# A convolution-and-transformer kernel: the 16-bit high part of the first activation is written by ScalarE instead of VectorE

## The chip, the core and the metric

One core of one Trainium2 chip runs the whole program. The metric is device time in microseconds (us), taken as the median of several executions. Busy times, starts and waits come from one profiled execution of the same kernel.

## What is computed

The program has two parts. The first turns 784 patches of 16x16 pixels with 3 colours (16 images of 7x7 patches) into tokens with a small residual convolution network; the second runs attention and MLP blocks over the tokens. The change touches the first part only:

```python
# 784 patches (bsz*h0*w0), each 3 x 16 x 16, normalized by its own mean and std
x = _conv2d(x, conv1_w, conv1_b)              # 3 -> 64 channels, 3x3
residual = x
x = _group_norm(x, gn1_g, gn1_b)              # 32 groups
x = jax.nn.gelu(x, approximate=False)         # <- the first activation
x = _conv2d(x, rconv1_w, rconv1_b)            # 64 -> 64 channels, 3x3
x = _group_norm(x, gn2_g, gn2_b)
x = jax.nn.gelu(x, approximate=False)
x = _conv2d(x, rconv2_w, rconv2_b)
x = residual + x
x = _conv2d(x, proj_w, proj_b, stride=P, pad=0)   # 64*16*16 -> 192 per patch
```

All is float32 in the reference. The kernel keeps the accuracy by splitting values into a 16-bit high part and a 16-bit low part, so that TensorE multiplies 16-bit numbers.

## The kernel before

**Stages.** From 0 to some 213 us the last convolution and the projection are folded into one matrix and the images are laid out. From some 213 to 1220 us the main stage runs over all patches. The rest, to 1526 us, is the tail with its transformer blocks. The change lies in the main stage.

**Tiling of the main stage.** A unit is 8 patches and there are 98 units. A unit has two halves q = 0, 1 of 4 patches each. A half is a *slot*, numbered k = 2u + q, so 196 slots; 14 units (28 slots) form a group, and there are 7 groups. The 128 partitions hold 64 channels times the two halves (even and odd rows) of a patch, and a slot's activation is 128 x 512 (4 patches x 128 pixels). Loops over pairs of units repeat the same four slots.

**One slot on each engine**, in the order in which the engine's own instruction list has it:

- TensorE (`emit`, L633): 30 matmuls of the 64 -> 64 convolution of slot k, in 15 pairs that use the two halves of the array at once. It first waits until the low part for slot k is there (`s_sp1`), after 6 pairs until the doubled high part has landed (`s_dup`), after 10 pairs it multiplies the statistics of slot k+3 (`means`, L602, waits for `s_ms`), after 13 pairs it does the first convolution (`conv1`, L592) into the bank that the gelu of slot k+2 must have left (`s_g1`). In all groups but the first the projection of the group before (`project`, L611) is woven between the pairs, from the fifth slot of the group on.
- VectorE (`slot`, L880): statistics of the two results (`channel_stats`, two times 4 instructions, L837), `moments` (L844 to L849), the low part of the second activation (`split2`, L877), `read_means` (L853 to L858), and last `split1` for slot k+2 (L868 and L870).
- GpSimd (`norm`, L388): turns the means into a scale and a shift for each patch, five small instructions (L394 to L404), of which the first is a power.
- ScalarE (`pair`, L489): the gelu of the second activation of slot k-3 (`gelu2_at`, 4 instructions, L477), its 16-bit high part (`hi2`, L485), and the gelu of the first activation of slot k+2 (`gelu1`, 4 instructions, L469). Each gelu needs a scale and shift of `norm`; the one of slot n of the first and the one of slot n-4 of the second use the same `norm(n)`.
- SyncE's queue (`double`, L292): four DMAs for a slot that copy the high part `hst[q]` into both partition halves of `acts[p]`, since every channel half is needed with both row halves. Between the slots stand loads of the image (`load_im`), of the projection's low weights (`load_chunk`), and at a group's end the stores of tokens.

**The split of the first activation.** The gelu writes `g1f` (float32). `split1` writes its 16-bit copy `hi` into `hst[q]`, with a border of zeros around each patch (rows of 16 written into rows of 18), signals `s_sp1h` (the doubling DMAs wait for it), and then writes `lo = g1f - hi` into `acts[p]`, which signals `s_sp1`:

```python
dve.wait_ge(s_g1, k + 1)                               # the gelu of slot k is done
if doubled is not None:
    dve.wait_ge(s_dup[1 - p][q], 64 * doubled)         # hst[q]'s last content has been copied on
v.tensor_copy(hi, src).then_inc(s_sp1h, 1)             # L868
dve.wait_ge(s_sp1h, k + 1)
v.tensor_tensor(lo, src, hi, ALU.subtract).then_inc(s_sp1, 1)   # L870
```

There are 198 such splits: 196 slots and two beyond the last.

Of the kernel before, what the change touches and what calls it, by code (L numbers as in the profile page):

```python
# [20 lines left out]
ALU, ACT = mybir.AluOpType, mybir.ActivationFunctionType  # L21

B, C, P, CH, E = 16, 3, 16, 64, 192
# [3 lines left out]
SL, WD = 9, 18  # L27
# [3 lines left out]
Q = 4  # L31
UNITS = NPAT // U
GU = 14
# [38 lines left out]
def build_front(nc, a, emb, xs, ts, wrd):  # L72
# [9 lines left out]
    with ExitStack() as ctx:  # L82
# [15 lines left out]
        g1f = f32q[:, 0:U * HALF].rearrange("p (g n) -> p g n", g=U)  # L98
        acts = [sb(f"acts_{i}", [128, 3, HB], F16) for i in range(2)]
        hfull = sb("hst", [128, U * PAD], F16)  # L100
        hst = [hfull[:, q * Q * PAD:(q + 1) * Q * PAD] for q in range(2)]
# [63 lines left out]
        s_scr, s_zero, s_padz = sem("x_stored"), sem("zero_tile"), sem("pads_zeroed")  # L165
# [258 lines left out]
        @block.scalar  # L424
        def _(act):
            def proj_hi(i, p, wait=True):
                n = 2 * i + p
                act.wait_ge(s_pld[p], 16 * (i + 1))
                if wait:
                    act.wait_ge(s_psp, n)  # L430
                    act.wait_ge(s_fdup, 64 * n)
                nc.scalar.activation(hfull[:, :].rearrange("p (r x) -> p r x", x=WD * Q)[:, :, Q:(P + 1) * Q],
                                     stage[p].rearrange("p (r x) -> p r x", x=P * Q), ACT.Copy, scale=WS).then_inc(s_psh, 1)

            def fold_step(i, p, first, more=True):
                n = 2 * i + p
                for q in range(2):
                    act.wait_ge(s_fold, 2 * n + q + 1)
                    nc.scalar.activation(whi[:, :, bass.ds(n * U + q * Q, Q)],
                                         rc[p][q][:, :].rearrange("p (n e) -> p n e", e=Q),  # L440
                                         ACT.Copy, scale=1.0 / WS).then_inc(s_whi, 1)
                if more:
                    proj_hi(i + 1, p)
                if not first:
                    act.wait_ge(s_ts[p], 32 * i)
                act.wait_ge(s_tps, n + 1)
                for k, bank in enumerate((c1[0], c1[1], pj)):
                    nc.scalar.activation(tev[p][:, :, 3 * P * k:3 * P * (k + 1)],
                                         bank[:, 0:192].rearrange("p (n e) -> p e n", e=Q),
                                         ACT.Copy, scale=1.0 / (WS * WS)).then_inc(s_tev, 1)  # L450

            act.wait_ge(s_padz, 2)
            proj_hi(0, 0, False)
            proj_hi(0, 1)
            for p in range(2):
                fold_step(0, p, True)
            with act.Fori(1, FU // 2 - 1) as i:
                for p in range(2):
                    fold_step(i, p, False)
            for p in range(2):  # L460
                fold_step(FU // 2 - 1, p, False, False)

            def gelu1(k, q, guard=True):

                act.wait_ge(s_sh, k + 1)
                if guard:
                    act.wait_ge(s_sp1, k - 1)
                for m in range(Q):
                    ins = nc.scalar.activation(g1f[:, q * Q + m, :], c1[q][:, m * HALF:(m + 1) * HALF], ACT.Gelu,  # L469
                                               bias=gsh[q][:, m:m + 1], scale=gsc[q][:, m:m + 1])  # L470
                ins.then_inc(s_g1, 1)

            def gelu2_at(u, q, p):
                act.wait_ge(s_sh, 2 * u + q + 5)
                act.wait_ge(s_sp2, 2 * u + q + 1)
                for m in range(Q):
                    ins = nc.scalar.activation(g2f[:, q * Q + m, :], rc[p][q][:, m * HALF:(m + 1) * HALF], ACT.Gelu,  # L477
                                               bias=gsh[q][:, Q + m:Q + m + 1],
                                               scale=gsc[q][:, Q + m:Q + m + 1])
                ins.then_inc(s_g2, 1)  # L480

            def hi2(u, q, buf, slot):

                act.wait_ge(s_g2, 2 * u + q + 5)
                nc.scalar.activation(g2[buf][:, 0, bass.ds(slot, Q), :], g2f[:, q * Q:q * Q + Q, :],  # L485
                                     ACT.Copy).then_inc(s_sp2h, 1)

            def group(g, b, first):
                def pair(u0, j, first, head):  # L489
                    for p in range(2):  # L490
                        u = u0 + p
                        for q in range(2):

                            if not (first and 2 * p + q < 3):
                                if head and 2 * p + q == 3:
                                    act.wait_ge(s_pj, 1 if first else g)
                                uu, qq, pp = (u - 2, 1, p) if q == 0 else (u - 1, 0, 1 - p)
                                gelu2_at(uu, qq, pp)
                                old = head and 2 * p + q < 3
                                hi2(uu, qq, 1 - b if old else b, slot2(j, p, q, old))  # L500
                            gelu1(2 * u + 2 + q, q)

                pair(g * GU, 0, first, True)
                with act.Fori(1, GU // 2) as j:
                    pair(g * GU + 2 * j, j, False, False)

            act.sem_inc(s_g2, 4)
            gelu1(0, 0, False)
            gelu1(1, 1, False)
            group(0, 0, True)  # L510
            act.wait_ge(s_wst, 16)
            with act.Fori(0, (GROUPS - 1) // 2) as i:
                group(2 * i + 1, 1, False)
                group(2 * i + 2, 0, False)
            for k in range(2 * UNITS - 3, 2 * UNITS):
                gelu2_at(k // 2, k % 2, k // 2 % 2)
                hi2(k // 2, k % 2, 0, (2 * GU + k - 2 * UNITS) * Q)
# [199 lines left out]
        def _(dve):  # L717
            v = nc.vector
# [138 lines left out]
                dve.wait_ge(s_mv, 2 * n + 2)  # L857
                v.tensor_tensor(mst[s][:, 1, :], mst[s][:, 1, :], msm[s][:, :], ALU.subtract).then_inc(s_rd, 1)  # L858

            def split1(k, q, p, doubled):  # L860

                dve.wait_ge(s_g1, k + 1)
                if doubled is not None:
                    dve.wait_ge(s_dup[1 - p][q], 64 * doubled)
                src = g1f[:, q * Q:q * Q + Q, :].rearrange("p g (r w) -> p g r w", w=P)
                hi = hst[q][:, :].rearrange("p (g r w) -> p g r w", g=Q, r=SL)[:, :, 1:9, 1:17]
                lo = acts[p][:, 2, q * Q * PAD:(q + 1) * Q * PAD].rearrange("p (g r w) -> p g r w", g=Q, r=SL)[:, :, 1:9, 1:17]
                v.tensor_copy(hi, src).then_inc(s_sp1h, 1)  # L868
                dve.wait_ge(s_sp1h, k + 1)
                v.tensor_tensor(lo, src, hi, ALU.subtract).then_inc(s_sp1, 1)  # L870

            def split2(k, q, buf, slot):
# [6 lines left out]
            def group(g, b, first):  # L879
                def slot(u, q, p, j, head, first):  # L880

                    pair_at = g * (GU // 2) + j

                    k = 2 * u + q
                    seen = not (first and p == 0 and q == 0)
                    if seen:
                        dve.wait_ge(s_rc, k)
                        channel_stats(1 - q, rc[p][0] if q == 1 else rc[1 - p][1], Q)
                    dve.wait_ge(s_c1, k + 5)
                    channel_stats(1 - q, c1[1 - q], 0)  # L890
                    moments(k + 3, 1 - q, 11 * k + 25 if seen else 25)
                    if not (first and p == 0) and not (first and p == 1 and q == 0):
                        old = head and 2 * p + q < 3
                        split2(k - 3, 1 - q, 1 - b if old else b, slot2(j, p, q, old))
                    read_means(k + 3, 1 - q)
                    split1(k + 2, q, 1 - p, pair_at + 1)

                def pair(u0, j, first, head):
                    for p in range(2):
                        for q in range(2):  # L900
                            if head and p == 1 and q == 1:
                                dve.wait_ge(s_pj, g if not first else 1)
                            slot(u0 + p, q, p, j, head, first)

                pair(g * GU, 0, first, True)
                with dve.Fori(1, GU // 2) as j:
                    pair(g * GU + 2 * j, j, False, False)
# [15 lines left out]
            moments(1, 1, 11)  # L923
            read_means(0, 0)
            read_means(1, 1)
            split1(0, 0, 0, None)
            dve.wait_ge(s_c1, 4)
            channel_stats(0, c1[0], 0)
            moments(2, 0, 18)
            read_means(2, 0)  # L930
            split1(1, 1, 0, None)
            group(0, 0, True)
            dve.wait_ge(s_wst, 16)
            with dve.Fori(0, (GROUPS - 1) // 2) as i:
# [747 lines left out]
```

## Time and profile before

| what | us |
|---|---|
| median of 3 runs | 1520.43 |
| lowest and highest of them | 1519.85, 1529.87 |
| the profiled execution | 1527.82 |
| its span, first to last instruction | 1526.0 |
| mean granted TensorE clock in it | 0.964 of full |
| PE (matmul) busy | 1378.1 (90%) |
| DVE (VectorE) busy | 1119.1 (73%) |
| ACT (ScalarE) busy | 860.6 (56%) |
| POOL (GpSimd) busy | 583.2 (38%) |

Busy times are those of the whole span. Since the stages differ, a share over the span says little about one stage; the rows further down are therefore cut by stage. "Idle before" an instruction is put down to what its engine waited for last. The names of engines in rows are PE (matmul), PEld (weight load), DVE, ACT, POOL and SPq (SyncE's queue).

### The profile page before, as it was taken

Reading aid. Unit: us, or ns where it says so; the run is one execution under the profiler, and the core shown is the slowest. Engines: PE = TensorE matmul, PEld = TensorE weight load, DVE = VectorE, ACT = ScalarE, POOL = GpSimd, SP = SyncE. Lnnn points to the kernel's source line nnn. Section 1 sums busy time; section 2 is a strip of 40 time slices with the busy share of each in tenths; the row PEclk is TensorE's granted clock in tenths of the full one; section 3 lists DMA queues with packets and bytes.
Section 4 is the critical chain, followed back from the end, with each engine's and each line's share of the span. In section 5 each row is a group of like instructions: output and inputs, shape, how many; then the busy total and the mean of one; then the engine's idle time right before and its main releaser. Section 6 shows DMA issues by size and latency. Waiting matters only on the chain. (4 is left out here: it accounts for less than half of the span.)

```text
span 1526.0 us, 43786 instructions
## 1 busy us (share of the span) xinstructions
PE 1378.1 (90%) x14026; PEld 1022.3 (67%) x14026; DVE 1119.1 (73%) x4210; ACT 860.6 (56%) x2126; POOL 583.2 (38%) x1114
## 2 busy tenths in 40 slices
PE   3999959888999999989999998999999785978889
PEld 1877523334888588768867885888578675655647
DVE  5753338999888988888898887888988743475630
ACT  1333426777676776667767676676666601333451
POOL 1000025555545545445454554544545401152600
PEclk9999979999999999999999999999999987977999
DMA  7899863334554555455545554555455596400000
GB/s 209 238 260 261 232 240 102 99 98 125 140 147 132 136 142 144 111 143 147 145 124 148 141 144 111 144 146 133 135 141 144 147 252 152 92 1 1 2 0 17
DMA packets 124565, 206.95 MB, mean 136 GB/s; under 512 B 19964, under 2 KB 88124, under 8 KB 123774
## 3 DMA queue, kind: packets, MB, share of 16 engines
q1 hardware_dynamic: 124414, 204.89, 49.8%
q8 instruction: 100, 1.64, 0.5%
q14 instruction: 51, 0.42, 0.1%
HBM read 103.70 MB, written 21.30 MB: 82 GB/s over the span
## 5 line engine op out<-in xcount | busy, mean ns | idle before, releaser
L540 PE MATMUL rc<-sb_acts,sb_rwd 128*64 128x512 f16 x1764 | 562.7, 392 | 20.2 <-DMA sb_acts<-sb_hst 19.5
L541 PE MATMUL rc<-sb_acts,sb_rwd 128*64 128x512 f16 x1764 | 563.7, 392 | 0.0
L394 POOL TENSOR_TENSOR sb_tmp<-sb_mst,sb_half_neg 128x8 f32<-128x8 f32 x200 | 353.9, 1770 | 471.5 <-DVE sb_mst L858 471.5
L469 ACT ACTIVATE sb_f32q<-c,sb_gsh,sb_gsc 128x128 f32<-128x128 f32 x792 | 298.3, 458 | 285.3 <-POOL sb_gsh L404 285.3
L540 PE MATMUL rc<-sb_acts,sb_rwl 128*64 128x512 f16 x1176 | 364.2, 392 | 5.3 <-issue 5.3
L541 PE MATMUL rc<-sb_acts,sb_rwl 128*64 128x512 f16 x1176 | 363.6, 391 | 0.0
L619 PE MATMUL pj<-sb_wall_arena 128*64 128x384 f16 x1792 | 306.0, 335 | 12.7 <-DVE sb_wall_arena L877 6.6
L477 ACT ACTIVATE sb_g2f<-rc,sb_gsh,sb_gsc 128x128 f32<-128x128 f32 x784 | 297.4, 482 | 4.5 <-POOL sb_gsh L404 4.5
L623 PEld LDWEIGHTS pj<-sb_wall_arena 128*64 128x64 f16 x1792 | 218.2, 223 | 66.1
L623 PE MATMUL pj<-sb_wall_arena 128*64 128x192 f16 x1792 | 238.7, 246 | 0.0
L540 PEld LDWEIGHTS rc<-sb_acts,sb_rwd 128*64 128x64 f16 x1764 | 179.8, 110 | 82.8 <-DMA sb_acts<-sb_hst 29.7
L619 PEld LDWEIGHTS pj<-sb_wall_arena 128*64 128x64 f16 x1792 | 215.0, 219 | 29.7 <-DMA sb_wall_arena<-w_lo 6.9
L560 PE MATMUL rc<-sb_acts,sb_wall_arena 128*64 128x512 f16 x720 | 165.5, 386 | 24.7 <-DVE sb_acts L748 15.2
L541 PEld LDWEIGHTS rc<-sb_acts,sb_rwd 128*64 128x64 f16 x1764 | 179.7, 110 | 5.1
L837 DVE BATCH_NORM_STATS2 sb_bn<-rc 128x6 f32<-128x128 f32 x784 | 173.7, 283 | 12.4 <-issue 5.4
L837 DVE BATCH_NORM_STATS2 sb_bn<-c 128x6 f32<-128x128 f32 x800 | 174.2, 278 | 0.0
L561 PE MATMUL rc<-sb_acts,sb_wall_arena 128*64 128x512 f16 x720 | 164.9, 385 | 0.0
L540 PEld LDWEIGHTS rc<-sb_acts,sb_rwl 128*64 128x64 f16 x1176 | 126.7, 109 | 48.6 <-issue 10.9
L877 DVE TENSOR_TENSOR sb_wall_arena<-sb_g2f,sb_wall_arena 128x512 f32 (+1 forms) x196 | 135.6, 692 | 31.0 <-issue 16.9
L870 DVE TENSOR_TENSOR sb_acts<-sb_f32q,sb_hst 128x512 f16<-128x512 f32 x198 | 137.8, 696 | 6.8
L485 ACT ACTIVATE sb_wall_arena<-sb_g2f 128x512 f32 (+1 forms) x196 | 124.8, 637 | 27.8 <-ACT sb_g2f L477 9.4
L541 PEld LDWEIGHTS rc<-sb_acts,sb_rwl 128*64 128x64 f16 x1176 | 126.7, 109 | 0.5
(171 smaller groups left out, 1888.2 us busy)
## 6 DMA issues: line engine op xcount, KB each, us to landing
sb_acts<-sb_hst SPq DMA_DIRECT2D x792, 78.8 KB, 2.6
sb_im<-x_planes SPq DMA_DIRECT2D x202, 136.5 KB
sb_wall_arena<-w_lo SPq DMA_DIRECT2D x48, 528.0 KB, 3.8
sb_acts<-sb_hst SPq DMA_DIRECT2D x96, 162.0 KB, 3.1
sb_wall_arena<-w_lo SPq DMA_DIRECT2D x24, 480.0 KB, 3.7
sb_f32q<-in_proj SPq DMA_DIRECT2D x12, 576.0 KB, 4.6
sb_wall_arena<-in_proj SPq DMA_DIRECT2D x12, 576.0 KB, 4.7
w_lo<-sb_wall_arena SPq DMA_DIRECT2D x1, 6144.0 KB, 20.7
```

The costliest lines, as they stand in the source:

```text
L394: ch.did(gp.tensor_tensor(t1, var, half_neg[:, :], ALU.pow))
L469: ins = nc.scalar.activation(g1f[:, q * Q + m, :], c1[q][:, m * HALF:(m + 1) * HALF], ACT.Gelu, bias=gsh[q][:, m:m + 1], scale=gsc[q][:, m ...
L477: ins = nc.scalar.activation(g2f[:, q * Q + m, :], rc[p][q][:, m * HALF:(m + 1) * HALF], ACT.Gelu, bias=gsh[q][:, Q + m:Q + m + 1], scale= ...
L540: nc.tensor.matmul(out[0:CH, :], w_odd, x_odd, start=(n == 0), stop=(n == 14))
L541: yield nc.tensor.matmul(out[CH:128, :], w_even, x_even, start=(n == 0), stop=(n == 14))
L560: nc.tensor.matmul(out[0:CH, :], w_odd, x_odd, start=(n == 0), stop=(n == 14))
L561: yield nc.tensor.matmul(out[CH:128, :], w_even, x_even, start=(n == 0), stop=(n == 14))
L619: last = nc.tensor.matmul(pj[at:at + 64, 0:2 * E], g2[b][:, 0, k:k + 64, n], both, start=(n == 0), stop=False)
L623: last = nc.tensor.matmul(pj[at:at + 64, 0:E], g2[b][:, 1, k:k + 64, n], whi[:, n, :], start=False, stop=(n == HALF - 1))
L837: v.bn_stats(bn6[s][:, at + m, :], src[:, m * HALF:(m + 1) * HALF]).then_inc(s_dch, 1)
L870: v.tensor_tensor(lo, src, hi, ALU.subtract).then_inc(s_sp1, 1)
L877: v.tensor_tensor(lo, src, hi, ALU.subtract).then_inc(s_sp2, 1)
```

## The change

The copy into `hst[q]` leaves `split1` and becomes a function of ScalarE, `hi1`, which follows each `gelu1`. The wait for the DMAs that read `hst[q]` (`s_dup`) goes with it. VectorE's `split1` keeps the subtraction only and waits for ScalarE's signal `s_sp1h` where it waited for the gelu. At the start ScalarE waits until the borders are zeroed.

```diff
+            def hi1(k, q, p, doubled):
+                if doubled is not None:
+                    act.wait_ge(s_dup[1 - p][q], 64 * doubled)
+                act.wait_ge(s_g1, k + 1)
+                src = g1f[:, q * Q:q * Q + Q, :].rearrange("p g (r w) -> p g r w", w=P)
+                nc.scalar.activation(hst[q][:, :].rearrange("p (g r w) -> p g r w", g=Q, r=SL)[:, :, 1:9, 1:17], src,
+                                     ACT.Copy).then_inc(s_sp1h, 1)
...
                             gelu1(2 * u + 2 + q, q)
+                            hi1(2 * u + 2 + q, q, 1 - p, g * (GU // 2) + j + 1)
...
             act.sem_inc(s_g2, 4)
+            act.wait_ge(s_padz, 2)
+            act.wait_ge(s_zl, 3)
             gelu1(0, 0, False)
+            hi1(0, 0, 0, None)
             gelu1(1, 1, False)
+            hi1(1, 1, 0, None)
...
-            def split1(k, q, p, doubled):
+            def split1(k, q, p):
 
-                dve.wait_ge(s_g1, k + 1)
-                if doubled is not None:
-                    dve.wait_ge(s_dup[1 - p][q], 64 * doubled)
+                dve.wait_ge(s_sp1h, k + 1)
                 src = g1f[:, q * Q:q * Q + Q, :].rearrange("p g (r w) -> p g r w", w=P)
...
-                v.tensor_copy(hi, src).then_inc(s_sp1h, 1)
-                dve.wait_ge(s_sp1h, k + 1)
                 v.tensor_tensor(lo, src, hi, ALU.subtract).then_inc(s_sp1, 1)
```

## Rows read from the trace of the kernel before

**Rows 1.** Windows, group 0 and groups 1 to 6: length, busy by engine, clock, DMA.

```profile
235.00:375.00 140.00, 123.90 (x1090) 53.21 (x1090) 129.43 (x543) 103.74 (x266) 75.48 (x150) 1.00 0.41 103
375.00:1211.00 836.00, 811.15 (x8978) 651.02 (x8978) 732.76 (x2964) 581.61 (x1480) 414.15 (x821) 0.99 0.51 138
```

**Rows 2.** The same windows, line L868 (VectorE's copy) alone: length, busy, count.

```profile
235.00:375.00 140.00, 12.83 (x30) 1.00 0.41 103
375.00:1211.00 836.00, 70.10 (x165) 0.99 0.51 138
```

**Rows 3.** Waits, 235 to 371 us: who waited for whom, us, times, longest.

```profile
PEld st L607 <- DVE sb_ms L849: 25.1, 29, 1.2
PEld c L598 <- ACT sb_f32q L469: 15.9, 26, 1.0
```

**Rows 4.** Waits, 371 to 1210 us.

```profile
PEld rc L540 <- DMA sb_acts<-sb_hst: 19.0, 23, 3.3
...
PEld st L607 <- DVE sb_ms L849: 13.6, 15, 1.4
```

**Rows 5.** Groups by line: names, shapes, count, busy us, mean ns, idle before.

```profile
L485 ACT ACTIVATE sb_wall_arena<-sb_g2f 128x512 f32 (+1 forms) x196 | 124.8, 637 | 27.8 <-ACT sb_g2f L477 9.4
L868 DVE CAST sb_hst<-sb_f32q 128x512 f16<-128x512 f32 x198 | 84.3, 426 | 3.8 <-ACT sb_f32q L469 3.3
...
L432 ACT ACTIVATE sb_hst<-sb_f32q 128x1152 f16<-128x1152 f32 x12 | 13.9, 1156 | 1.7 <-DMA sb_acts<-sb_hst 1.7
```

**Rows 6.** Timeline, 282 to 292 us (group 0): start, length, engine, line, idle before.

```profile
282.17 0.17 DVE L858 TENSOR_TENSOR sb_mst<-sb_mst,sb_msm 128x8 f32<-128x8 f32 x1
...
282.42 1.75 POOL L394 TENSOR_TENSOR sb_tmp<-sb_mst,sb_half_neg 128x8 f32<-128x8 f32 x1 [1.90 <-DVE sb_mst L858]
...
282.71 0.69 DVE L870 TENSOR_TENSOR sb_acts<-sb_f32q,sb_hst 128x512 f16<-128x512 f32 x1
...
283.75 0.63 ACT L485 ACTIVATE sb_wall_arena<-sb_g2f 128x512 f32 x1 [0.22 <-ACT sb_g2f L477]
...
285.17 1.50 ACT L469 ACTIVATE sb_f32q<-c,sb_gsh,sb_gsc 128x128 f32<-128x128 f32 x4 [0.79 <-POOL sb_gsh L404]
...
286.83 0.17 DVE L858 TENSOR_TENSOR sb_mst<-sb_mst,sb_msm 128x8 f32<-128x8 f32 x1
...
287.41 0.69 DVE L870 TENSOR_TENSOR sb_acts<-sb_f32q,sb_hst 128x512 f16<-128x512 f32 x1
...
290.08 1.50 ACT L469 ACTIVATE sb_f32q<-c,sb_gsh,sb_gsc 128x128 f32<-128x128 f32 x4 [1.25 <-POOL sb_gsh L404]
```

**Rows 7.** Timeline, 856 to 864 us (group 4), ScalarE and VectorE.

```profile
856.30 1.50 ACT L469 ACTIVATE sb_f32q<-c,sb_gsh,sb_gsc 128x128 f32<-128x128 f32 x4 [1.18 <-POOL sb_gsh L404]
...
858.51 0.42 DVE L868 CAST sb_hst<-sb_f32q 128x512 f16<-128x512 f32 x1
...
858.97 0.70 DVE L870 TENSOR_TENSOR sb_acts<-sb_f32q,sb_hst 128x512 f16<-128x512 f32 x1
...
859.34 0.64 ACT L485 ACTIVATE sb_wall_arena<-sb_g2f 128x512 f32 x1
...
861.52 1.51 ACT L469 ACTIVATE sb_f32q<-c,sb_gsh,sb_gsc 128x128 f32<-128x128 f32 x4 [1.54 <-POOL sb_gsh L404]
...
862.05 0.69 DVE L877 TENSOR_TENSOR sb_wall_arena<-sb_g2f,sb_wall_arena 128x512 f32 x1
...
863.97 0.70 DVE L870 TENSOR_TENSOR sb_acts<-sb_f32q,sb_hst 128x512 f16<-128x512 f32 x1
```

**Rows 8.** Timelines of GpSimd and VectorE, 250 to 256 us (group 0).

```profile
254.20 1.64 POOL L394 TENSOR_TENSOR sb_tmp<-sb_mst,sb_half_neg 128x8 f32<-128x8 f32 x1 [1.49 <-DVE sb_mst L858]
...
254.36 0.43 DVE L868 CAST sb_hst<-sb_f32q 128x512 f16<-128x512 f32 x1 [0.24 <-ACT sb_f32q L469]
```

**Rows 9.** Timeline of SyncE's queue, 645 to 656 us (start of group 3).

```profile
649.17 5.05 SPq L296 DMA_DIRECT2D sb_acts<-sb_hst  x8
```

**Rows 10.** Timeline of VectorE, 650 to 652 us (start of group 3).

```profile
651.14 0.43 DVE L868 CAST sb_hst<-sb_f32q 128x512 f16<-128x512 f32 x1
```

More of the change, by code:

```diff
@@ L880, in slot @@
                 def slot(u, q, p, j, head, first):
-                    pair_at = g * (GU // 2) + j
                     k = 2 * u + q
@@ L895, in slot @@
                     read_means(k + 3, 1 - q)
-                    split1(k + 2, q, 1 - p, pair_at + 1)
+                    split1(k + 2, q, 1 - p)
                 def pair(u0, j, first, head):
@@ L925, in _ @@
             read_means(1, 1)
-            split1(0, 0, 0, None)
+            split1(0, 0, 0)
             dve.wait_ge(s_c1, 4)
@@ L930, in _ @@
             read_means(2, 0)
-            split1(1, 1, 0, None)
+            split1(1, 1, 0)
             group(0, 0, True)
```

## The prediction

> **What bounds the kernel now.** I read the windows by stage first, then the waits in each, then the timeline of single slots. Only the main stage holds the edited instructions, and it has two regimes. In group 0 (235 to 375 us) there is no projection to weave in: 30 copies lie in 140 us, so a slot takes 140 / 30 = 4.67 us [rows 2], VectorE is busy 129.43 of 140 us (92%) and TensorE 123.90 [rows 1]. There TensorE waits for VectorE's statistics (25.1 us in 29 waits) and for the first gelu (15.9 us in 26) [rows 3]. In groups 1 to 6 (375 to 1211 us) a slot takes 836 / 165 = 5.07 us [rows 2], and TensorE is busy 811.15 of 836 us (97%), VectorE 732.76 (88%), ScalarE 581.61 (70%) [rows 1]. TensorE's statistics wait is down to 13.6 us over 165 slots, and its largest wait is for the doubling DMAs, 19.0 us [rows 4]. So TensorE sets the slot in 165 of some 196 slots, and what VectorE gains or loses there is cover. ScalarE idles 1.18 and 1.54 us ahead of its first gelu there [rows 7]: room for one more instruction.
>
> The reader should not take the 92% in group 0 for the whole answer. Behind it stands a loop with latency that spans two slots: `read_means(n)` on VectorE, `norm(n)` on GpSimd, `gelu1(n)` on ScalarE, `split1(n)` on VectorE, then VectorE's statistics, moments, `split2`, and `read_means(n+2)`. Its pieces in group 0 [rows 6]: end of L858 at 282.17 + 0.17 = 282.34 to the gelu at 285.17 is 2.83 us, the next time 287.00 to 290.08 = 3.08; mean 2.95. The gelu takes 1.50. From the start of L870 (282.71) to the end of the next L858 (287.00) is 4.29, all of it VectorE work. What is left of two slots, 9.33 - 2.95 - 1.50 - 4.29 = 0.59 us, is the time from the gelu's end to the start of L870: the copy of 0.43 and small gaps. The loop is almost tight before the change.
>
> **Removed on VectorE.** The copy: 426 ns x 198 = 84.3 us of busy time [rows 5]. In groups 1 to 6 this lies beside a TensorE at 97%, so it is worth nothing by itself. In group 0 it would be worth 0.43 x 30 = 12.8 us if nothing took its place.
>
> **Added on ScalarE.** The trace has no Copy from `g1f` into `hst` by ScalarE. The nearest row is `hi2`, the same size and function, 637 ns [rows 5]. The padded destination can be judged from L432, which writes that same tile with borders: 1152 elements in 1156 ns [rows 5]. The step from 512 to 1152 elements is 519 ns for 640, or 0.81 ns an element, with no sign of a price for borders. So I take 0.64 us; the lower end is 0.60 and the upper end 1.16, the whole of L432's row. Before it comes the wait for the gelu's own end, as before `hi2`: 0.22 us [rows 6]. So the high part is there 0.86 us after the gelu's end, where VectorE had it 0.43 us after it at best.
>
> **ScalarE's own cycle.** In the main stage it works from 856.30 to 859.34 + 0.64 = 859.98, that is 3.68 us, and starts again at 861.52 [rows 7]. With 0.22 + 0.64 added it works 4.54 us of 5.07 and is free at 860.84, still 0.68 us before its next gelu. So the first gelu is not delayed, nor is TensorE's `conv1` behind it. Behind the new instruction on ScalarE stand `gelu2` and `hi2`, for which VectorE's `split2` and, a slot later, TensorE wait; they come 0.86 us later. VectorE's `split2` (L877) started at 862.05, 2.07 us behind the end of `hi2` at 859.98 [rows 7], so they stay hidden. If that cover were gone, each 0.1 us would cost 16.5 us over 165 slots.
>
> **The moved wait.** `s_dup` asks for the DMAs of two slots earlier. TensorE passes the same semaphore in mid-slot, before VectorE's `read_means`, so VectorE never waited for it. ScalarE meets it up to a microsecond earlier. It costs nothing except where the DMAs are late for TensorE too (23 waits, 19.0 us [rows 4]), and there the slot is already lost. No DMA is added, and SyncE's queue keeps its order.
>
> **Groups 1 to 6, regular slots.** Gelu ends at 857.80, high part at 858.66, L870 can start 0.08 us later (the gap with which POOL follows L858, 282.34 to 282.42 [rows 6]), at 858.74; it started at 858.97 [rows 7]. The next slot: 863.03 + 0.94 = 863.97, the same as before [rows 7]. So VectorE neither gains nor loses; the bill there is 0. The high part itself is ready at 858.66 instead of 858.93, or in the other slot 863.89; the doubling DMAs follow within some tenths of the old time and are needed more than a slot later.
>
> **Starts of groups 1 to 6.** Behind the tokens' stores SyncE's queue is late and issues eight doublings back to back, 649.17 to 654.22 [rows 9]. VectorE's copy in this stretch ran at 651.14 to 651.57 [rows 10], and the second four issues followed it at once. If VectorE's copy stood directly behind the gelu, the high part now comes later by 0.86 - 0.43 = 0.43 us, and TensorE is waiting for these DMAs (up to 3.3 us [rows 4]). Six starts x 0.43 = +2.6 us; the bounds are 0, where the queue is the later one, and twice that.
>
> **Group 0.** The loop becomes 2.95 + 1.50 + (0.22 + 0.64 + 0.08) + 4.29 = 9.68 us for two slots, 4.84 a slot. One term may shrink: GpSimd's power starts just after VectorE's copy and takes 1.75 us [rows 6]; the one at 254.20 takes 1.64, and there the copy began only at 254.36 [rows 8]. With the copy gone and VectorE idle at that moment, I take 1.64: 9.57, or 4.785 a slot. Cost: (4.785 - 4.67) x 30 = +3.5 us; +5.2 with the power as it is. VectorE alone could go at 4.67 - 0.43 = 4.24, but it now waits some 0.5 us a slot at L870.
>
> The Trainium skill (GPSIMD Engine Reference, Key points) says that GpSimd shares its SBUF interfaces with VectorE and contends with instructions in a 2-port mode or with two SBUF inputs. By that rule the power gets its 1.64 us only while L870, which has two SBUF inputs, is not running; the power at 254.20 had the copy beside it and was short, so the start seems to matter, not the overlap. By the rule in full the sum would be the +5.2, by the row +3.5.
>
> **Sum.** 3.5 + 2.6 = +6.1 us. Against the profiled execution (1527.82, of which 1526.0 is span) that is 1533.9; it was 7.4 us longer than the median, so for the median 1520.43 + 6.1 = 1526.5 us.
>
> **The rivals.**
>
> *VectorE's relief carries.* If the high part were no later for VectorE than before, group 0 falls by up to 12.8 us, and the shorter VectorE slot also takes some of the 13.6 us of statistics waits. For it: VectorE at 92%, TensorE's 25.1 us of waits. Against: the loop above, which has 0.59 us for what now needs 0.94. Time: 1520.4 - 12.8 = 1507.6, still within 1%; only with most of the 13.6 us added does it pass 1% (15.2 us). 12%.
>
> *ScalarE becomes the bound (slower).* The place is ScalarE's cycle. It decides when that cycle s passes the point where 165 (s - 5.07) + 30 (s - 4.67) = 15.2, which is s = 5.09, a Copy of 0.64 + (5.09 - 4.54) = 1.19 us, or a small Copy and 0.5 us of waits. At 0.1 us more, s = 5.19: +19.8 + 15.6 = +35, 1556. Against: both Copy rows fit 0.81 ns an element. 7%.
>
> *The doubling DMAs come late everywhere.* If the later high part in the slots with little slack delays landings that TensorE waits for, a price of 0.4 us in half of the 165 slots is +33; more likely in the 23 places that already wait: 23 x 0.4 = +9, with group 0 1533. For: the waits exist. Against: in 142 of 165 slots TensorE finds the DMAs landed [rows 4]. 11%.
>
> **How the numbers follow.** The forecast has 70%, with its own range from 1520 (no cost: the power and the hand-over both shorter) to 1531 (5.2 + 2.6, and 2.4 for a Copy of 0.8 us). The rest is 12, 7 and 11%. The range over all, holding 8 in 10, goes from 1511 to 1539: it leaves out the full relief and ScalarE as the bound. About 1% is what a measurement of this kernel can tell from no change: faster by over 1% (below 1505.2) 4%, the strongest part of the relief; slower by over 1% (above 1535.6) 12%, ScalarE's case and half of the DMAs'; within 1% 84%.
>
> **What would show each step right or wrong.** The new ScalarE row at 0.60 to 0.68 us, 198 times, behind an idle of about 0.2 us. L870 in group 0 with a new wait for ScalarE, about 0.5 us in each slot, and a group 0 slot of 4.75 to 4.85 us. VectorE's busy time down by 84 us, ScalarE's up by 126. TensorE still at 97% from 375 to 1211 us, with slots of 5.07 to 5.10. The power at 1.64 us. Wrong would be: group 0 slots under 4.6 us (the loop does not bind), ScalarE with no wait for GpSimd left (it is the bound), or TensorE's waits for the doubling DMAs well above 30 us.

## The result

| | before | after |
|---|---|---|
| median, us | 1522.3 (10 runs, 1517.15 to 1529.95) | 1538.05 (10 runs, 1532.97 to 1540.25) |
| profiled execution, us | 1527.82 | 1538.50 |
| ratio | | 1.0089, 95% interval 1.007 to 1.0108 |

The changed kernel is slower: by 0.9% (13.5 us) in the ratio, by 15.75 us in the medians. The forecast was 1526.5 us, +6.1 us. Its direction was right and its size less than half of the measured one. The median of 1538.05 us lies outside the forecast's own range (1520 to 1531) and just inside the range over all (1511 to 1539). Part of that distance is the starting point: the forecast was added to 1520.43 us, and over all ten runs the kernel before has a median of 1522.3.

The two profiled executions differ by 10.7 us only. That is because the one of before was a long one: from the last subtraction to the last projection matmul it took 59.7 us, but 51.4 us in the changed kernel and 51.5 to 55.6 us in the kernels of the experiments. Up to the last subtraction of the main stage (1211.1 us before, 1227.9 after) the changed kernel is 16.8 us longer, and there lies the loss.

Windows of the kernel after, all engines: length, busy (count) of PE, PEld, DVE, ACT, POOL, clock, DMA share, GB/s.

```profile
235.00:375.00 140.00, 116.21 (x1030) 52.46 (x1028) 112.00 (x483) 113.95 (x278) 76.34 (x141) 0.99 0.37 93
375.00:1211.00 836.00, 802.70 (x8856) 639.56 (x8854) 666.54 (x2777) 676.46 (x1629) 423.72 (x815) 1.00 0.51 137
```

The same windows, the subtraction (L879) alone:

```profile
235.00:375.00 140.00, 19.44 (x28) 0.99 0.37 93
375.00:1211.00 836.00, 112.93 (x163) 1.00 0.51 137
```

Against [rows 1, 2]: in group 0 28 splits instead of 30 in 140 us, so 5.0 us a slot instead of 4.67; in the rest 163 instead of 165. VectorE is down from 129.4 to 112.0 us and from 732.8 to 666.5, in part because fewer slots lie in these windows. Over the whole span its busy time fell by 72.0 us (1119.1 to 1047.1), not by the 84 us of the copy's row, since neighbouring instructions overlap at their edges. The relief is there, and it has bought nothing.

Groups by line, kernel after; they answer to [rows 5] and [rows 6]:

```profile
L478 ACT ACTIVATE sb_hst<-sb_f32q 128x512 f16<-128x512 f32 x198 | 127.5, 644 | 21.8 <-DMA sb_acts<-sb_hst 4.0
L879 DVE TENSOR_TENSOR sb_acts<-sb_f32q,sb_hst 128x512 f16<-128x512 f32 x198 | 137.2, 693 | 77.3 <-ACT sb_hst L478 75.5
L394 POOL TENSOR_TENSOR sb_tmp<-sb_mst,sb_half_neg 128x8 f32<-128x8 f32 x200 | 366.3, 1832 | 469.5 <-DVE sb_mst L871 469.5
```

ScalarE's copy takes 644 ns, as forecast, and VectorE now waits 75.5 us for it. The new thing is the third row: GpSimd's power, untouched by the change, takes 1832 ns in the mean instead of 1770, where 1640 was forecast. The mean hides two populations: 106 powers of 1.64 or 1.65 us and 94 of 2.01 to 2.19 us. Of the 94, 93 meet the subtraction L879. The last power of the kernel meets the other subtraction instead, the one of the second activation, and the kernel before has the same case at the same place, the only one of its 200 powers above 1.91 us:

```profile
1215.80 1.29 DVE L877 TENSOR_TENSOR sb_wall_arena<-sb_g2f,sb_wall_arena 128x512 f16<-128x512 f32 x2
```

```profile
1215.96 2.02 POOL L394 TENSOR_TENSOR sb_tmp<-sb_mst,sb_half_neg 128x8 f32<-128x8 f32 x1 [2.54 <-DVE sb_mst L858]
```

Timeline of one pair of slots in group 0, kernel after, columns as in [rows 6]:

```profile
304.02 0.17 DVE L871 TENSOR_TENSOR sb_mst<-sb_mst,sb_msm 128x8 f32<-128x8 f32 x1
...
304.27 1.64 POOL L394 TENSOR_TENSOR sb_tmp<-sb_mst,sb_half_neg 128x8 f32<-128x8 f32 x1 [1.14 <-DVE sb_mst L871]
...
305.51 0.70 DVE L879 TENSOR_TENSOR sb_acts<-sb_f32q,sb_hst 128x512 f16<-128x512 f32 x1 [1.32 <-ACT sb_hst L478]
...
306.78 0.20 POOL L404 TENSOR_TENSOR sb_gsh<-sb_wid,sb_tmp 128x8 f32<-128x8 f32 x1
307.08 0.63 ACT L493 ACTIVATE sb_wall_arena<-sb_g2f 128x512 f32 x1 [0.22 <-ACT sb_g2f L485]
307.62 1.49 ACT L469 ACTIVATE sb_f32q<-c,sb_gsh,sb_gsc 128x128 f32<-128x128 f32 x4
...
309.20 0.64 ACT L478 ACTIVATE sb_hst<-sb_f32q 128x512 f16<-128x512 f32 x1
309.63 0.17 DVE L871 TENSOR_TENSOR sb_mst<-sb_mst,sb_msm 128x8 f32<-128x8 f32 x1
...
309.87 0.69 DVE L879 TENSOR_TENSOR sb_acts<-sb_f32q,sb_hst 128x512 f16<-128x512 f32 x1
309.88 2.18 POOL L394 TENSOR_TENSOR sb_tmp<-sb_mst,sb_half_neg 128x8 f32<-128x8 f32 x1 [2.90 <-DVE sb_mst L871]
```

Slots no longer follow each other evenly: subtractions start 4.36 us apart (305.51 to 309.87), then 5.6 to 6.2. In the first slot VectorE waits 1.32 us for the high part. In the second the shift is ready at 306.98, but ScalarE is in `hi2` until 307.71 and the gelu starts 0.64 us late; the high part then comes just as VectorE ends its means, the subtraction starts at 309.87, the power at 309.88, and the power takes 2.18 us. In the following, such a power is called hit.

Waits, 375 to 1211 us, kernel after; they answer to [rows 4]:

```profile
DVE sb_acts L879 <- ACT sb_hst L478: 51.7, 83, 1.9
...
PEld rc L553 <- DMA sb_acts<-sb_hst: 23.5, 30, 2.9
PEld c L611 <- ACT sb_f32q L469: 14.0, 14, 1.8
```

In the following, a group's length is the time from one subtraction's start to that of the 28th after it (for the last group, to the last one, the 27th).

| us | group 0 | groups 1 to 6 | together |
|---|---|---|---|
| before | 130.7 | 849.2 | 979.9 |
| after | 139.5 | 857.7 | 997.2 |

Of groups 1 to 6, the slots 9 to 22 of each took 426.2 us before and 426.3 after. The 8.5 us are lost in the first eight slots (240.7 to 246.0) and the last six (182.3 to 185.4).

### The profile page after: what moved, and what is told of

Its sections match the earlier page's. It is cut to its first block and busy times, and to the rows that moved or that the text cites. A ratio compares the mean times of both kernels' runs of the same rounds, so it can differ in the third digit from the quotient of the medians.

```text
span 1536.7 us, 43835 instructions
## 1 busy us (share of the span) xinstructions
PE 1383.5 (90%) x14026; PEld 1018.6 (66%) x14026; DVE 1047.1 (68%) x4012; ACT 982.9 (64%) x2324; POOL 601.9 (39%) x1114
## 3 DMA queue, kind: packets, MB, share of 16 engines
q8 instruction: 100, 1.64, 0.5%
## 5 line engine op out<-in xcount | busy, mean ns | idle before, releaser
L394 POOL TENSOR_TENSOR sb_tmp<-sb_mst,sb_half_neg 128x8 f32<-128x8 f32 x200 | 366.3, 1832 | 469.5 <-DVE sb_mst L871 469.5
L485 ACT ACTIVATE sb_g2f<-rc,sb_gsh,sb_gsc 128x128 f32<-128x128 f32 x784 | 291.0, 451 | 3.7 <-POOL sb_gsh L404 3.5
L636 PEld LDWEIGHTS pj<-sb_wall_arena 128*64 128x64 f16 x1792 | 220.4, 223 | 66.5
L632 PEld LDWEIGHTS pj<-sb_wall_arena 128*64 128x64 f16 x1792 | 219.6, 219 | 22.2 <-DVE sb_wall_arena L886 6.7
L879 DVE TENSOR_TENSOR sb_acts<-sb_f32q,sb_hst 128x512 f16<-128x512 f32 x198 | 137.2, 693 | 77.3 <-ACT sb_hst L478 75.5
L553 PEld LDWEIGHTS rc<-sb_acts,sb_rwl 128*64 128x64 f16 x1176 | 127.2, 109 | 50.1 <-issue 13.5
L478 ACT ACTIVATE sb_hst<-sb_f32q 128x512 f16<-128x512 f32 x198 | 127.5, 644 | 21.8 <-DMA sb_acts<-sb_hst 4.0
```

The lines of the kernel that those rows point to most:

```text
L394: ch.did(gp.tensor_tensor(t1, var, half_neg[:, :], ALU.pow))
L553: nc.tensor.matmul(out[0:CH, :], w_odd, x_odd, start=(n == 0), stop=(n == 14))
L632: last = nc.tensor.matmul(pj[at:at + 64, 0:2 * E], g2[b][:, 0, k:k + 64, n], both, start=(n == 0), stop=False)
L636: last = nc.tensor.matmul(pj[at:at + 64, 0:E], g2[b][:, 1, k:k + 64, n], whi[:, n, :], start=False, stop=(n == HALF - 1))
```

## The experiments

**Group 0 alone, and groups 1 to 6 alone.** Which stage pays? In the first run ScalarE copies in group 0 and ahead of it, in the second in groups 1 to 6.

```diff
-                            hi1(2 * u + 2 + q, q, 1 - p, g * (GU // 2) + j + 1)
+                            if zero:          # first run; "if not zero" in the second
+                                hi1(2 * u + 2 + q, q, 1 - p, g * (GU // 2) + j + 1)
...
+                    split1(k + 2, q, 1 - p, g * (GU // 2) + j + 1, not zero)   # VectorE copies elsewhere; "zero" in the second
```

> The new arrangement (ScalarE copies) in group 0 and ahead of it only, VectorE copies as before in groups 1 to 6. Theory A (two losses: group 0 is a loop bound by latency, where the changed kernel's trace has 4.98 us a slot instead of 4.67, and the starts of the other groups lose 1 to 3 us each): group 0 takes some 139 us again instead of 131, groups 1 to 6 their old lengths, the whole +8 us, ratio 1.005 to 1.006. Theory B (the loss is ScalarE's fuller schedule everywhere, mostly in groups 1 to 6): under +3 us, ratio 1.002 or less.

Measured: ratio 1.0035 (1.002 to 1.005); group 0 139.4 us, groups 1 to 6 847.2.

> The other part alone: VectorE copies in group 0, ScalarE copies in groups 1 to 6. Theory A: group 0 back at 131 us; in groups 1 to 6 the regular slots stay at 10.1 us a pair and only the first slots of each group are later, 8 us together, ratio 1.004 to 1.006. Theory B: most of the 13 to 16 us is here, ratio 1.009. The prediction had +2.6 us for this part.

Measured: ratio 1.0025 (1.0008 to 1.0042); group 0 131.0 us, groups 1 to 6 854.4 (slots 9 to 22: 426.4). Both parts pay, group 0 8.7 us and the others 5.2 here and 8.5 in the changed kernel. Theory A was right that there are two losses and that the middle slots pay nothing beside a busy TensorE. Its ratios were high by 0.15% or more, and it had the second loss in the first slots of a group only, where the last six take part (182.3 to 184.2 us). The two ratios together give 0.6% where the whole change gave 0.9%; the intervals just allow it.

**A gap in front of the subtraction.** In the changed kernel the hit powers all belong to subtractions that start at or before the power. A fill of a spare tile by VectorE should move the subtraction behind the power's start.

```diff
             def split1(k, q, p):
+                v.memset(dum[:, :], 0.0)      # 128x256 float32; 128x400 in the second run
                 dve.wait_ge(s_sp1h, k + 1)
```

> The changed kernel with a fill of 128x256 (0.27 us by VectorE's other fills) put ahead of VectorE's wait for the high part. In the changed kernel's trace GpSimd's power takes 1.64 us where VectorE's subtraction starts 0.1 us or more behind the power's start, and 2.02 to 2.19 us where the subtraction is already running. Theory A (this collision is part of the loss): with the gap all powers take 1.64 to 1.76 us and group 0 falls from 139.5 to 135 us or less although VectorE does 0.27 us more in each slot; ratio to before 1.004 to 1.006. Rival (the collision is only a mark, the late high part is the whole cost): the powers get shorter, group 0 stays at 139 us or grows, ratio 1.009 or more.

Measured: ratio 1.0144 (1.0109 to 1.0178), group 0 139.9 us. The expected gain did not come, and the reason stands in the timeline of this kernel:

```profile
309.85 0.27 DVE L876 MEMSET sb_dum<- 128x256 f32 x1
310.04 0.63 DVE L881 TENSOR_TENSOR sb_acts<-sb_f32q,sb_hst 128x512 f16<-128x512 f32 x1
```

```profile
309.93 2.23 POOL L395 TENSOR_TENSOR sb_tmp<-sb_mst,sb_half_neg 128x8 f32<-128x8 f32 x1 [2.90 <-DVE sb_mst L872]
```

With the fill directly ahead of it the subtraction hits the power although it starts 0.11 us behind the power's start: 90 powers took 2.23 us. So this edit made the collision worse and cannot say what the kernel is without it.

> As the gap before, with a fill of 128x400 instead of 128x256. The first gap (0.19 us in effect) put the subtraction's start 0.12 us behind the power's start, and there 90 powers took 2.23 us, the worst of all: it moved the collision instead of removing it. This one puts it some 0.24 us behind. Theory A: the powers are 1.64 us in all slots, group 0 falls to 137 us or less from 139.5 although VectorE does 0.39 us more in each slot. Rival: the power's length follows the overlap with the subtraction wherever it lies, so powers stay at 2 us or more in some 90 slots, and group 0 at 139 us or above.

Measured: ratio 1.0166 (1.012 to 1.0212), group 0 141.6 us, 81 powers of 2.38 us though the subtraction starts 0.26 us behind the power. The rival's numbers came, and both gap runs failed as a remedy. Two cases of this kernel, each with ScalarE's copy, the power and the subtraction:

```profile
351.66 0.64 ACT L479 ACTIVATE sb_hst<-sb_f32q 128x512 f16<-128x512 f32 x1
...
352.34 2.38 POOL L395 TENSOR_TENSOR sb_tmp<-sb_mst,sb_half_neg 128x8 f32<-128x8 f32 x1 [2.90 <-DVE sb_mst L872]
...
352.60 0.63 DVE L881 TENSOR_TENSOR sb_acts<-sb_f32q,sb_hst 128x512 f16<-128x512 f32 x1
...
371.81 0.64 ACT L479 ACTIVATE sb_hst<-sb_f32q 128x512 f16<-128x512 f32 x1
...
372.41 1.64 POOL L395 TENSOR_TENSOR sb_tmp<-sb_mst,sb_half_neg 128x8 f32<-128x8 f32 x1 [2.64 <-DVE sb_mst L872]
...
372.67 0.63 DVE L881 TENSOR_TENSOR sb_acts<-sb_f32q,sb_hst 128x512 f16<-128x512 f32 x1
```

In both the subtraction starts 0.26 us behind the power. In the first the high part that it waits for was ready 0.04 us ahead of the power's start (352.30), and the power is hit; in the second it came 0.04 us behind (372.45), and the power is not. The same division holds in all fourteen traces of this study, whichever engine copies: the 689 powers that this subtraction hit started 0.027 us or more after the high part of the next subtraction was ready, and none of the other 2097 did. So what decides is when the subtraction could go, not where its recorded start lies. No run was made to test this rule; it was read from the traces afterwards.

**The same useless work on ScalarE, ahead of the high part and behind it.** This separates the path from ScalarE's load. The Copy took 0.42 us ahead of the high part and 0.40 us behind it (medians).

```diff
                 act.wait_ge(s_g1, k + 1)
+                nc.scalar.activation(dum..., zeros... (128x256), ACT.Copy)      # first run
...
                                      ACT.Copy).then_inc(s_sp1h, 1)
+                nc.scalar.activation(dum..., zeros... (128x256), ACT.Copy)      # second run instead
```

> The changed kernel with one more Copy of 128x256 on ScalarE (some 0.43 us, estimated from 644 ns for 512 elements at 0.81 ns an element) between the gelu and the high part's copy; its result is used by nothing. It lengthens both ScalarE's cycle (4.37 to 4.8 us a slot) and the path from the gelu to the subtraction (0.77 to 1.2 us). Theory A (the two-slot loop R(n), norm, gelu, high part, subtraction, R(n+2) sets group 0): 9.36 + 0.43 us for two slots at the least, 4.9 a slot, plus what the collision with GpSimd's power adds: group 0 137 to 146 us. In groups 1 to 6 the loop comes to 9.8 to 10.2 us against TensorE's 10.13: +5 to +20 us there. Theory O (ScalarE's busy schedule alone): the same as the run with the Copy behind.

Measured: ratio 1.0076 (1.0047 to 1.0106), group 0 137.3 us, groups 1 to 6 857.3.

> The same additional Copy, but behind the high part's copy: ScalarE's cycle grows to 4.8 us, the path from gelu to subtraction stays 0.77 us. Theory A with the collision: in group 0 of the changed kernel every other subtraction is ready just as VectorE is free and runs into the start of GpSimd's power (2.13 to 2.18 us instead of 1.64); a ScalarE cycle of 4.8 us moves it away from there, so group 0 does not grow by 0.43 us a slot: 134 to 140 us against 139.5, and groups 1 to 6 stay within 5 us. Theory O: group 0 grows by 28 x 0.43 = 12 us to some 151 us, like the run with the Copy ahead.

Measured: ratio 1.0031 (1.0005 to 1.0058), group 0 133.1 us, groups 1 to 6 856.7. This is the plainest result of the study: 198 useless copies made the changed kernel some 9 us faster. From 235 to 371 us 1 of 29 powers was hit where 11 of 28 had been. Theory O, by which ScalarE's load sets the time, is refuted. Timeline, run with the Copy behind:

```profile
301.72 0.17 DVE L874 TENSOR_TENSOR sb_mst<-sb_mst,sb_msm 128x8 f32<-128x8 f32 x1
...
301.96 1.64 POOL L395 TENSOR_TENSOR sb_tmp<-sb_mst,sb_half_neg 128x8 f32<-128x8 f32 x1 [1.97 <-DVE sb_mst L874]
302.37 0.69 DVE L882 TENSOR_TENSOR sb_acts<-sb_f32q,sb_hst 128x512 f16<-128x512 f32 x1 [0.49 <-ACT sb_hst L479]
```

In group 0 most slots now look like this one, 4.6 to 4.8 us apart: ScalarE's longer cycle spaces the gelus evenly, the high part comes behind the power's start, and the power is left alone. The two runs also give the price of the path. In both all powers between 235 and 371 us but one are short, and the median time from the gelu's end to the subtraction is 1.07 and 0.76 us; group 0 differs by 4.2 us in 28 slots, 0.15 us a slot for 0.31 us of path: one half, as a loop over two slots asks.

**Two and three patches by ScalarE, the rest by VectorE.**

```diff
-                nc.scalar.activation(hst[q]...[:, :, 1:9, 1:17], src, ACT.Copy).then_inc(s_sp1h, 1)
+                nc.scalar.activation(hst[q]...[:, 0:2, 1:9, 1:17], src[:, 0:2], ACT.Copy).then_inc(s_hs, 1)
...
+                v.tensor_copy(hi[:, 2:4], src[:, 2:4]).then_inc(s_sp1h, 1)     # VectorE, once the gelu is done
+                dve.wait_ge(s_sp1h, k + 1)
+                dve.wait_ge(s_hs, k + 1)
                 v.tensor_tensor(lo, src, hi, ALU.subtract).then_inc(s_sp1, 1)
```

> ScalarE copies two of the four patches and VectorE the other two, at the same time. The high part should be whole some 0.1 + 0.43 us behind the gelu; VectorE saves 0.18 us a slot. Theory A: the loop is 2.95 + 1.5 + 0.57 + 4.29 = 9.3 us without a collision, so group 0 is 130 to 131 us as before the change, and the time within 0.3% of before; a gain is worth at most 2 to 3 us. Theory B (any copy on ScalarE costs): group 0 135 us or more.

Measured: ratio 0.9975 (0.9952 to 0.9999), group 0 130.9 us, groups 1 to 6 850.2; in the groups no power takes more than 1.79 us, and 187 of 195 take less than 1.7.

> ScalarE copies three of the four patches, VectorE one (some 0.2 us, in front of the subtraction). The path from gelu to subtraction grows over the run with two and two by some 0.1 us (0.42 to 0.54 us of Copy). Theory A: what matters is the path and whether VectorE's subtraction runs as GpSimd's power starts; a short copy stands in front of it, so no power takes 2 us, and the loop is some 9.5 us: group 0 131 to 134 us. Rival (the power is hit wherever the subtraction follows VectorE's other work closely, as behind the fills): powers of 2 us and group 0 at 137 us or more.

Measured: ratio 0.9982 (0.9959 to 1.0005), group 0 132.4 us, groups 1 to 6 847.1. The timelines of VectorE and of GpSimd in this kernel:

```profile
306.76 0.17 DVE L873 TENSOR_TENSOR sb_mst<-sb_mst,sb_msm 128x8 f32<-128x8 f32 x1
306.88 0.23 DVE L883 CAST sb_hst<-sb_f32q 128x128 f16<-128x128 f32 x1
307.14 0.69 DVE L886 TENSOR_TENSOR sb_acts<-sb_f32q,sb_hst 128x512 f16<-128x512 f32 x1
```

```profile
307.01 1.64 POOL L396 TENSOR_TENSOR sb_tmp<-sb_mst,sb_half_neg 128x8 f32<-128x8 f32 x1 [2.42 <-DVE sb_mst L873]
```

Here the path from the gelu to the subtraction is no shorter than in the changed kernel (median 0.79 us in group 0 against 0.76, and 0.89 against 0.77 in groups 1 to 6), and ScalarE does three quarters of the added work. But the subtraction waits for VectorE's own short copy, which in every slot ends 0.06 us or more behind the power's start; no power of the groups takes 2 us. Group 0 is 7.1 us and groups 1 to 6 are 10.6 us shorter than in the changed kernel. A shorter path cannot be the reason.

**ScalarE only beside the projection.** If the loss in groups 1 to 6 is only in slots where TensorE has no projection, VectorE's copy in the first four slots of each group should end it.

```diff
-                            hi1(2 * u + 2 + q, q, 1 - p, g * (GU // 2) + j + 1)
+                            if not (zero or head):
+                                hi1(2 * u + 2 + q, q, 1 - p, g * (GU // 2) + j + 1)
```

> ScalarE copies only in the slots of groups 1 to 6 where TensorE has projection matmuls woven in (24 of 28); VectorE copies in group 0 and in the first four slots of each group, where there is none. Theory A (ScalarE's copy costs only where TensorE does not set the slot): groups 1 to 6 come back from 854 to 857 us to within 2 us of the 847 to 850 us that kernels with VectorE's copy show, and group 0 is 131 us: same as before, ratio 1.000 to 1.003. Rival (the loss in groups 1 to 6 is that of late doublings or of ScalarE's schedule in any slot): groups 1 to 6 stay at 854 us or more, ratio 1.004 or more.

Measured: ratio 1.0048 (1.0016 to 1.008), group 0 133.2 us, groups 1 to 6 856.0. The first eight slots of the groups are back at 240.5 us (240.7 before), but the last six take 187.7 (182.3 before). The expectation's rival has the numbers (ratio and groups 1 to 6), but the verdict on the place is open: the edit also puts one more wait in front of each copy on the engine that does it, and even group 0, where VectorE copies as before, is 2.5 us longer.

**A useless VectorE copy in front of the subtraction.** Is it the copy that guards the power?

```diff
             def split1(k, q, p):
+                dve.wait_ge(s_g1, k + 1)
+                v.tensor_copy(dum[:, :], g1f[:, q * Q + Q - 1, :])     # 128x128; first run
+                v.tensor_copy(dum[:, :], zeros[:, :])                  # 128x8, no wait; second run instead
                 dve.wait_ge(s_sp1h, k + 1)
```

> The changed kernel (ScalarE writes all of the high part) with one useless VectorE copy of 128x128 from the gelu's result to a spare tile in front of VectorE's wait: 0.23 us a slot more on VectorE, and the same in front of the subtraction as in the run with three patches by ScalarE and one by VectorE. Theory A (the loss is mostly that the subtraction, started right behind VectorE's means, holds up GpSimd's power; a copy in between lets the power start): no power of 2 us, group 0 132 to 134 us instead of 139.5, groups 1 to 6 847 to 851 us instead of 857.6, ratio 0.998 to 1.003, so faster than the changed kernel although it does more. Rival (the later high part is the loss; the run with three patches was faster only for its 0.1 us shorter copy): group 0 137 us or more, ratio 1.007 or more.

> The same with the smallest copy there is, 128x8 (0.1 us or less), in that place. If any instruction between the means and the subtraction lets the power start, then no power of 2 us and group 0 at 131 to 134 us as above. If the subtraction must start 0.1 to 0.2 us behind the power, as the fills suggest, the tiny copy leaves it at -0.1 to 0.1 us and the powers that it hits take 2.0 to 2.2 us: group 0 137 to 140 us, ratio 1.007 or more.

Measured: ratio 1.0137 (1.0098 to 1.0175) and 1.0114 (1.009 to 1.0138); group 0 141.3 and 141.0 us; groups 1 to 6 857.8 and 855.0. Theory A of the first expectation failed. VectorE and GpSimd in the first of these kernels:

```profile
310.22 0.17 DVE L872 TENSOR_TENSOR sb_mst<-sb_mst,sb_msm 128x8 f32<-128x8 f32 x1
310.30 0.22 DVE L877 CAST sb_dum<-sb_f32q 128x128 f16<-128x128 f32 x1
310.46 0.70 DVE L882 TENSOR_TENSOR sb_acts<-sb_f32q,sb_hst 128x512 f16<-128x512 f32 x1
```

```profile
310.47 2.18 POOL L395 TENSOR_TENSOR sb_tmp<-sb_mst,sb_half_neg 128x8 f32<-128x8 f32 x1 [2.90 <-DVE sb_mst L872]
```

The copy is as long as with three patches, but nothing waits for its end, so the subtraction follows 0.16 us behind the copy's start instead of 0.26, that is 0.01 us ahead of the power, and hits it. It is the moment at which the subtraction could go that counts, not what stands in between. Over the two kernels all 183 powers whose subtraction started between 0.10 us ahead of them and their own start took 2.09 to 2.19 us; all whose subtraction started 0.01 us or more behind took 1.64. Beside the kernel with three patches this is the closest pair of the study: the same short VectorE copy ahead of the subtraction, waited for there and not here, a ScalarE copy of 0.54 us there and 0.64 here, no power hit there and 94 here; 132.4 against 141.3 us in group 0, 847.1 against 857.8 in groups 1 to 6.

**The half-and-half kernel once more.**

> The kernel with two patches by each engine once more, to measure it against the kernel before. Its trace shows group 0 at 130.9 us and groups 1 to 6 at 850.2 us, before 130.7 and 849.2: by these rows no gain, ratio 0.998 to 1.001. If the 0.9975 of the first time was real, it comes again at 0.998 or below.

Measured: ratio 0.9974 (0.9954 to 0.9993), group 0 131.1 us, groups 1 to 6 848.1. Twice some 4 us faster than the kernel before, just clear of the noise. Its groups together take 979.2 us against 979.9, so the profiles do not show where the 4 us come from; what they can show is that it does not lose.

## Why the prediction was right and wrong

**The loop over two slots: right.** The slope (half of a change of path for a slot) and the level both hold. From [rows 6] the old path was 0.59 us in the mean; with 0.76 us and no collision the slope gives 28 x 0.17 / 2 = +2.4 us for group 0, and the two kernels nearest to that state gave +2.4 (Copy behind) and +1.7 (three patches, where the path of 0.79 us would give +2.8). The 0.11 us by which their powers are shorter, 1.5 us by the same slope, does not show in it. VectorE's relief (72.0 us measured, 84 forecast) was worth nothing in groups 1 to 6, as forecast, nor in group 0.

**The hand-over: too long in the sum, by 0.18 us.** I took 0.22 + 0.64 + 0.08 = 0.94 us; measured are 0.09 + 0.64 + 0.03 = 0.76 us (gelu's end at 309.11, copy from 309.20 to 309.84, subtraction at 309.87). The 0.22 us of idle ahead of `hi2` is not the price of waiting for one's own gelu in general. With this term alone the forecast for group 0 falls from +3.5 to +0.8 us.

**The power: the failed step.** I wrote that the power would shrink from 1.75 to 1.64 us "with the copy gone and VectorE idle at that moment". In nearly every second slot VectorE is not idle: the high part is already there, nothing stands between the means and the subtraction any more, and the subtraction runs into the power's start. The other powers did shrink to 1.64 us, but the hit ones take 2.01 to 2.19: 0.26 to 0.44 us more than the 1.75 of before, where I had 0.11 less. With the 0.64 us that the gelu waits for ScalarE in the other slot, both chains of the loop come to some 9.9 us: 139.5 us for group 0. Taking the collision away, by even spacing or by letting the subtraction wait for a copy that ends behind the power's start, takes 6.3 and 7.1 of the 8.8 us away. How much of the 8.8 us is the longer power and how much ScalarE's 0.64 us no run separates, for in both remedies the slots are also spaced more evenly.

I had put a rule beside this step: the Trainium skill (GPSIMD Engine Reference, Key points) says that GpSimd contends with VectorE instructions that have two SBUF inputs. The subtraction is one, and the traces agree, with 2.01 to 2.19 us against 1.64. I had weighed the rule against the power at 254.20 [rows 8], from which the start seemed to matter and not the overlap. That reading holds. But I put VectorE as idle at that start, and by the rule in full I had a power of 1.75 us as the worst, where the trace of before held one of 2.02 us, the last, shown above with its subtraction.

**ScalarE's cycle: right in regular slots, wrong in group 0.** In the slots timed above it measured 4.37 us (303.25 to 307.62), under my 4.54, but with slots in pairs of 4.3 and 5.6 us a mean of 4.98 no longer tells whether ScalarE is free: it was late by 0.64 us for every other gelu.

**Groups 1 to 6: regular slots right, the rest under-sized.** Slots 9 to 22 changed by 0.1 us over six groups. For the starts I had +2.6 us; the loss is 5 to 8 us, in the first eight and the last six slots of the groups. TensorE waits 14.0 us for the first gelu at its weight loads (6.3 before) and 23.5 us for the doublings (19.0). The kernel with three patches by ScalarE, which has no hit power, takes 847.1 us there. So a late high part alone, as late there, does not cost it, and the hit powers are the likely cause. That is not shown slot by slot: the run with the Copy behind had 60 of them here instead of 78 and lost 7.5 us, the one with the Copy ahead only 22, on a path 0.3 us longer, and lost 8.1.

**The rivals.** VectorE's relief did not carry, and ScalarE did not become the bound. Late doublings show 4.5 us of added waits at TensorE's weight loads and 2.2 us at its matmuls (11.5 to 13.7), less than the 9 us of that rival.

**What stays open:** why a subtraction that could go before the power holds it up even where a fill delays its start; why the last six slots of a group lose; where the half-and-half kernel gains its 4 us.

## What to carry to other kernels

An instruction that leaves an engine also leaves a gap in time: look at which instruction moves up into its place, and what runs on other engines at that moment. Judge such a meeting by when the instruction could go, its last wait, and not by its recorded start alone. Where a loop with latency is tight, price the moved work by the path (here half a microsecond a slot for each microsecond, since the loop spans two slots) and not by the engine's busy time. And compare spacings slot by slot: a mean of 4.98 us hid an alternation of 4.3 and 5.6 with a different delay in either slot.

## What the runs showed of the hardware

- GpSimd's power on 128x8 elements takes 1.64 us alone, and 2.01 to 2.19 us where a VectorE subtraction with two inputs in SBUF (128x512) starts between 0.17 us ahead of it and its own start. A hit power ends 1.47 to 1.52 us after the end of the subtraction, in all 689 cases. Where the subtraction starts 0.01 us or more behind, there is no effect, unless it was ready before and another VectorE instruction delayed it, as the fill did (2.23 and 2.38 us). The edge is sharp: with the high part ready 0.027 us or more before the power's start it was always hit, with 0.026 us or less never.
- A VectorE copy of float32 (128x512) that starts just ahead of the power and ends behind its start costs it 0.12 us (1.754 against 1.637 us by the medians of before and after). In the kernel before such a power ends 1.49 to 1.50 us after the end of the copy (1.75 to 1.90 us long), much as a hit power does after the subtraction. The copies of one patch in the kernel with three patches are too short to show (powers of 1.64 us, but for one of 1.72).
- The short GpSimd instruction behind the power is hit too: L395 at 305.87 took 0.39 us instead of 0.20 while the subtraction of 305.51 was running, and 7 of the 200 in the changed kernel took 0.39 us or more.
- ScalarE's Copy of 128 x 256, 384 and 512 elements into the bordered tile took 0.43, 0.54 and 0.64 us (medians), about 0.8 ns for each further element of a partition.
